# One-hots of the second neighbour sum: from two ScalarE steps to one GpSimd comparison

## What is computed

```python
def _rgcn(x, edge_index, edge_type, weight, root, bias):
    src, dst = (edge_index[0], edge_index[1])
    msgs = x[src]
    out = x @ root + bias
    for r in range(weight.shape[0]):
        mask = (edge_type == r).astype(x.dtype)
        sums = jax.ops.segment_sum(msgs * mask[:, None], dst, num_segments=n)
        cnt = jax.ops.segment_sum(mask, dst, num_segments=n)
        mean = sums / jnp.maximum(cnt, 1.0)[:, None]
        out = out + mean @ weight[r]
    return out
u = _rgcn(x, edge_index, edge_type, weight, root, bias)
z = jnp.concatenate([u, x], axis=1) @ w_gate + b_gate
h = jnp.tanh(u) * z + x * (1.0 - z)
```

## Time and profile before

| What | us |
|---|---|
| Median of 3 runs (2558.67, 2566.13, 2567.54) | 2566.13 |
| Span of the profiled execution (first to last instruction) | 2555.3 |
| TensorE busy in that span | 2387.4 |
| VectorE, ScalarE, GpSimd busy | 1562.8, 919.0, 871.2 |
| The second neighbour sum, first gather to last slot | about 1724 to 2130 |

### The profile page before, as it was taken

How to read it: one execution, slowest core, us unless ns; L and a number is a source line. 1 busy time by engine, 2 the same in 40 slices (tenths; PEclk the granted TensorE clock), 3 DMA queues, 4 the chain that set the end, 5 groups by cost and what they waited for, 6 DMA issues and landing times.

```text
span 2555.3 us, 29106 instructions
## 1 busy us (share of the span) xinstructions
PE 2387.4 (93%) x9625; PEld 1691.6 (66%) x9625; DVE 1562.8 (61%) x2417; ACT 919.0 (36%) x1629; POOL 871.2 (34%) x843
## 2 busy tenths in 40 slices
PE   6989998969999979999999999999999897986998
PEld 3543334634444458788888888888778686875786
DVE  8737777431142377645545545547889898766655
ACT  4012223311111233222222212217889896534333
POOL 2767774001111035555600000014445552112444
PEclk9999999979999989999999999999999998997999
DMA  4026776273342265453453353357778885447875
GB/s 156 2 97 205 206 208 170 107 260 111 99 132 98 72 224 221 166 191 131 140 202 124 135 209 124 127 185 251 245 257 297 280 298 209 158 149 272 313 278 192
DMA packets 195724, 466.10 MB, mean 182 GB/s; under 512 B 29353, under 2 KB 30153, under 8 KB 195609
## 3 DMA queue, kind: packets, MB, share of 16 engines
q1 hardware_dynamic: 101192, 219.34, 24.6%
q0 software_dynamic: 64272, 190.20, 23.2%
q10 hardware_dynamic: 30144, 55.12, 5.7%
HBM read 370.23 MB, written 99.96 MB: 184 GB/s over the span
## 4 chain that ended last, share of the span: by engine, by line
PE 82%; DMA 7%; DVE 5%; issue 2%; ACT 2%; POOL 1%; DVEq 0%; SPq 0%; ACTq 0%; POOLq 0%
PE pair L1292 9%; PE pair L1293 8%; PE pair L1294 8%; PE pair L1172 6%; PE pair L1192 6%; PE pair L1079 4%; PE pair L1310 3%; PE pair L1313 3%; PE pair L1330 3%; PE pair L1332 3%; PE pair L1331 3%; PE pair L1039 3%; PE pair L1058 3%; DMA XT<-h_rows,l_src 2%; PE pair L1017 2%
## 5 line engine op out<-in xcount | busy, mean ns | idle before, releaser
L1471 ACT ACTIVATE sq_h<-quad 128x512 fp32r<-128x512 f32 x196 | 122.9, 633 | 453.6 <-PE pair L1294 448.8
L1292 PE MATMUL pair<-sq_h,xh 128*128 128x512 f32 x700 | 273.5, 391 | 4.3 <-DVE sq_l L2290 4.3
L1293 PE MATMUL pair<-sq_h,xl 128*128 128x512 f32 x700 | 273.2, 390 | 0.0
L1294 PE MATMUL pair<-sq_l,xh 128*128 128x512 f32 x700 | 273.1, 390 | 0.0
L932 POOL DMA_INDIRECT rows_y<-y_rows,l_row x184 | 201.2, 1093 | 206.0 <-PE pair L1313 178.9
L2378 DVE SCALAR_TENSOR_TENSOR low_y<-rows_y,l_inv,high_y 128x1024 fp32r<-128x1024 f32 x184 | 233.8, 1283 | 41.3 <-ACT high_y L1471 41.0
L1471 ACT ACTIVATE high_y<-rows_y,l_inv 128x1024 fp32r<-128x1024 f32 x184 | 210.4, 1143 | 35.7 <-PE pair L1313 25.7
L909 POOL DMA_INDIRECT inv_ring<-inv_count,at_ring x184 | 189.0, 1027 | 74.6 <-issue 56.3
L872 POOL DMA_INDIRECT XT<-h_rows,l_src x184 | 178.6, 971 | 68.5 <-issue 37.2
L2290 DVE TENSOR_TENSOR sq_l<-quad,sq_h 128x512 fp32r<-128x512 f32 x196 | 131.5, 696 | 99.3 <-ACT sq_h L1471 98.5
L1079 PE MATMUL pair<-XT,XN 128*128 128x504 f32 x368 | 188.5, 636 | 0.0
(11 more groups left out here) (369 smaller groups left out, 5037.7 us busy)
## 6 DMA issues: line engine op xcount, KB each, us to landing
quad<-in_L_gnn_weight SPq DMA_DIRECT2D x28, 1024.0 KB, 5.6
xh<-sum_parts SPq DMA_DIRECT2D x14, 1280.0 KB, 7.4
xl<-sum_parts SPq DMA_DIRECT2D x14, 1280.0 KB, 11.0
y_rows<-u ACTq DMA_DIRECT2D x70, 256.0 KB, 2.2
tok_raw<-in_L_ffn_w SPq DMA_DIRECT2D x8, 2048.0 KB, 13.6
tok_raw<-in_L_ffn_w SPq DMA_DIRECT2D x16, 1024.0 KB, 13.0
exp_bg<-bias_gelu_rows SPq DMA_DIRECT2D x23, 512.0 KB, 5.0
x_rows<-X SPq DMA_DIRECT2D x20, 512.0 KB, 6.4
```

The costliest lines, as they stand in the source:

```text
L1292: mm(o, high[:, k, :], sq_h[:, k, :], start=(k == 0), stop=False)
L1293: mm(o, low[:, k, :], sq_h[:, k, :], start=False, stop=False)
L1294: last = mm(o, high[:, k, :], sq_l[:, k, :], start=False, stop=(k == KE - 1))
L1471: return nc.scalar.activation(dst, src, func, **kw)
```

## The change

ScalarE's lines 1728 and 1736 go, with `row_off`, its semaphore and its waits. GpSimd makes the one-hot of a slot with one instruction, `tensor_scalar` with `is_equal`: the column numbers `iota_free` compared with the slot's target row. It stands in front of the gather of the slot three further on, behind the wait that the gather had already; the last three stand behind all gathers. Sizes of rings, the gathers and the work of TensorE and VectorE are unchanged.

```diff
-        high_ready, low_ready, row_off_ready, hot01_ready = sem("high_ready"), sem("low_ready"), sem("row_off_ready"), sem("hot01_ready")
+        high_ready, low_ready, hot01_ready = sem("high_ready"), sem("low_ready"), sem("hot01_ready")
...
+            def one_hot(s):
+                if s >= HOTS:
+                    pool.wait_ge(slot_summed, RING0 + SLOTS + s - HOTS + 1)
+                pool.tensor_scalar(hot01[:, s % HOTS, :], iota_free[:, 0:P], l_row[:, s:s + 1], None, ALU.is_equal).then_inc(hot01_ready, 1)
+
             for s in range(SLOTS):
                 if s >= RING1:
                     pool.wait_ge(slot_summed, RING0 + SLOTS + s - RING1 + 1)
+                if s >= HOTS - 1:
+                    one_hot(s - HOTS + 1)
                 pool.indirect_dma_start(rows_y[s % RING1][:], None, y_rows,
                                         bass.IndirectOffsetOnAxis(ap=l_row8[:, s:s + 1], axis=0)
                                         ).then_inc(y_in[s % RING1], 16)
+            for s in range(SLOTS - HOTS + 1, SLOTS):
+                one_hot(s)
...
             for s in range(SLOTS):
-                if s >= 1:
-                    act.wait_ge(hot01_ready, s)
-                nc.scalar.activation(row_off[:], iota_free[:, 0:P], ACT.Abs, bias=l_row[:, s:s + 1], scale=-1.0).then_inc(row_off_ready, 1)
                 act.wait_ge(*y_here(s))
                 if s >= 3:
                     act.wait_ge(slot_summed, RING0 + SLOTS + s - 2)
                 copy(high_y[s % 3][:], rows_y[s % RING1][:], scale=l_inv[:, s:s + 1]).then_inc(high_ready, 1)
-                act.wait_ge(row_off_ready, s + 1)
-                if s >= HOTS:
-                    act.wait_ge(slot_summed, RING0 + SLOTS + s - HOTS + 1)
-                nc.scalar.activation(hot01[:, s % HOTS, :], row_off[:], ACT.Relu, bias=ones[:, 0:1], scale=-1.0).then_inc(hot01_ready, 1)
```

More of the change, by code:

```diff
@@ L269, in build @@
         gate0_half = place("gate0_half", "hot", [P, HALF], skip=HOTS * P)
-        row_off = place("row_off", "sel", [P, P])
         uh = place("uh", "w", [P, 2, KD, P], F32R)
```

## The result

| | before | after |
|---|---|---|
| Median of 4 runs, us | 2566.4 | 2623.5 |
| Lowest and highest | 2558.7, 2567.5 | 2619.2, 2636.9 |
| Span of the profiled execution | 2555.3 | 2622.9 |

The changed kernel is slower: its time is 1.023 of that before, 95% interval 1.0194 to 1.0266, or 57 us. The interval is clear of 1; whether the loss is above 2% it leaves open. The forecast was 2591.1, 25 us slower. The sign held, and GpSimd is the bound as forecast; the size was off by more than a factor of two.

The account below looks back on a forecast made before the run. TensorE was taken to bound the stage before, GpSimd units 2 and 3 after: 26 us lost less 1 gained makes 25; the span of 2555.3 becomes 2580.3, plus 10.8 for the median gives 2591.1 us, range 2562 to 2637.

Parts of the forecast that it names:

- What bounds, what it removes: Sum stage: TensorE bounds, GpSimd looks idle; dropping ScalarE's two steps gains 1 us, at unit changes and in units 2, 3.
- What it adds: GpSimd: 184 comparisons of 128 columns at 0.29 us, upper bound 0.45; with 0.15 us issue gap, 0.44 us per slot.
- What holds it: GpSimd: each comparison waits for a running low_y, 0.41 us on average, 0.35 in longer slots; 42 of 184 gathers already held.
- The sum per slot: GpSimd's need against spare time: units 2 and 3 over by 0.26 and 0.37 us per slot, 11 and 16.5 us, taken as 26.
- Unit 1 fits, and unit 0: GpSimd in units 0 and 1: unit 1's need of 0.80 us per slot fits its spare 0.99, unit 0 likewise; no loss.
- The range: Whole kernel time from 2562 to 2637 us, taking in most of the no-change case and the lower part of the heavy one.
- heavy rival: Second rival, GpSimd: comparison 0.45 us, gather held as often, 0.41 us more; 70 to 75 us slower, some 2637; chance 0.15.
- No change: First rival: GpSimd and VectorE fall into step, or queues absorb holds; -1 to +10 us, some 2570; chance 0.36 including fourth rival.
- Queues of three and four slots: Part of the no-change rival: slots saved up between GpSimd, ScalarE and TensorE absorb the holds on GpSimd.
- Faster: Third rival: ScalarE's lateness caused all TensorE waits outside the cover and GpSimd keeps up; -14.8 us, 2551; chance 0.03.
- The signs to look for: Units 2 and 3: gathers well over 1.09 us or comparisons far over 0.3, GpSimd not waiting for sums, high_y waiting for gathers.
- The last sign: GpSimd: comparisons of 0.6 us or more that nothing holds would point to the second, heavier rival.

Follow-up runs that it names:

- memset run: Changed kernel with GpSimd's comparison replaced by a memset of the same 128 columns, one-hots left all zeros: 2557.4 us against 2565.0 before, stage 396.5 us.
- first trace of before: The kernel before, unedited, in its first profiled trace: stage of the sum 397.7 us; a later repeat on the third chip gave 407.4.
- copy run: Changed kernel with the comparison replaced by a 128-column copy, one-hots left out: stage 419.1 us, whole 2736.8 us against 2723.9 before on that chip.
- first pair of traces: Kernel before and changed kernel, unedited, first traced: stages 397.7 and 468.6 us; the second pair, repeated on the third chip, gave 407.4 and 466.2.
- one-input run: Changed kernel with low_y made from rows_y alone, subtraction left out, so that step has one SBUF input: 2575.7 us against 2565.0 before, stage 401.8.
- VectorE's one-hots: Kernel with one-hots made by VectorE in front of low_y, ScalarE's two steps gone, GpSimd only gathering: 2720.3 us against 2723.9 before, ratio 0.9993, stage 403.0.

## Why the prediction was right in its reasons and wrong in its size

- **What bounds, what it removes.** Right as far as it can be seen: inside a unit TensorE waited for nobody, and freeing ScalarE gave next to nothing. The memset run's stage is 1 us shorter than the first trace of before, well inside the spread, so the 1 us itself is not shown.
- **What it adds.** This is the step that failed: "I take 0.29", with 0.45 as the upper bound. The comparison takes 0.61 us, above both. The row of the select was one instruction of another form, the copies were another form too, and I took the two-input sum as a ceiling by its slope per column, though the changed form has a fixed part of its own. A smaller miss is in the gather: behind a comparison it takes 1.01 us unheld, not 0.94 (behind a memset 0.94, behind a copy 0.96). A third goes the other way and was hidden: the working takes 0.30 us in front of each gather and 0.15 behind the comparison, 0.45 in all, but a gather that follows a comparison no longer follows a gather. Measured are 0.17 and 0.04, so 0.24 us per slot were counted too much.
- **What holds it.** Right in kind. The hold was put at 0.35 to 0.41 us per comparison; measured are 1.03 - 0.61 = 0.42. That is nearer than the rule behind it deserves: at the 2.53 us that a slot took, a chance arrival would give 1.31/2.53 x 0.63 = 0.33 us. Arrivals are not by chance; in the copy run they made the hold 0.57. The gathers are held 0.27 us on average, where they were held 0.16 before; I had them unchanged. The count of 42 gathers needs a word: by the recorded times 126 start inside a `low_y`. Those that start 0.13 to 0.98 us into it are the 42, and each ends 0.81 us behind its end; 14 that start in its first 0.07 us and 70 that start in its last 0.15 us are not held.
- **The sum per slot.** With 0.61 in place of 0.29, and 0.07 more for the gather, the same working gives for units 2 and 3 an excess of 0.26 + 0.32 + 0.07 = 0.65 and 0.76 us, so 50 x 0.65 - 2 = 30.5 and 50 x 0.76 - 2 = 36 us, and for units 0 and 1, 0.80 + 0.39 - 0.99 = 0.20 us, 3.6 and 5.6 us: 76 us in all against 71 measured in the first pair of traces and 59 in the second. By units it fits less well: measured are 24.9 and 26.9, 8.5 and 9.2. Part of the agreement is luck. The 0.24 us of gaps counted too much stand against 0.07 us of hold on the comparison and 0.11 on the gather that are missing; with all three units 2 and 3 come to an excess of 0.59 and 0.70 us, 27.5 and 33 us. And with the right gaps but the price of 0.29 and the holds as forecast, unit 2 would have been over by 0.02 us and unit 3 by 0.13 us, and the forecast would have been close to no change. With the copy, whose length was the one I used, the stage was 419.1 us, 12 to 21 above the two of before, where the sum had 25: there, too, a hold of 0.57 us in place of 0.35 made up for the gaps. "Unit 1 fits, and unit 0" fell with the comparison's price.
- **The range.** The time lies inside it, above the 2579 to 2615 us that I had given the forecast. Its upper end, 2637, is the heavy rival, which had a longer comparison; but its 0.45 us was still too short, and its other half, a gather held as often as the comparison, came out at 0.27 us in place of 0.41. It is the nearest of the four, and I had given it 0.15.
- **The other rivals.** No change was what the stages of the one-input run and of VectorE's one-hots gave (401.8 and 403.0 us); it needed either no holds or another engine. Queues of three and four slots did absorb the gathers' holds in the memset run, but not both holds and the comparison. Faster falls: without ScalarE's two steps and with one-hots for nothing, TensorE still waited 18.1 of 19.2 us for `low_y`.
- **The signs to look for.** They were there: gathers of 1.28 us, comparisons far over 0.3, hardly a wait of GpSimd for sums, `high_y` waiting for the gather's DMA. The last sign was there as well, the one of the second rival, for the comparison takes 0.61 us where nothing holds it.

## What to carry to other kernels

Before work goes to an idle engine, price the very form of the instruction, with its operands and size, by a probe: another form of the same size was off by a factor of two here, and the sum hung on it. Then ask who shares something with that engine: idle time per turn has to hold the new instruction and the holds it will meet, and here the comparison's length without holds cost next to nothing (one-input run), a short instruction with its holds 12 to 21 us (copy), both together 59 to 71 us. Count also what the gaps between instructions become when their order changes. Where a GpSimd instruction must run beside VectorE steps with two inputs in SBUF, try cutting these steps shorter: in this kernel one trace showed most of the loss gone.

## What the runs showed of the hardware

- On GpSimd a `tensor_scalar` of 128 columns takes 0.61 us (0.53 with a constant), for both operations tried and with its output rounded or not (0.60); a copy of the same size takes 0.29, a memset 0.21.
- A VectorE step with two tensor inputs in SBUF holds GpSimd's comparisons, copies and gathers until 0.13 us before its recorded end (held comparisons end 0.48 us behind it, held gathers of the kernel before 0.81); a gather that starts in its first 0.07 us is not held (14 in the kernel before). The same columns with one input in SBUF hold none of 184 gathers (1.03 us at most), and of 184 memsets, which read nothing, none was held in the memset run (0.23 us at most).
- The other direction is cheap here: `low_y` took 1.31 us on average in the changed kernel in place of 1.28, though 184 comparisons of 0.61 us ran beside it.
- A gather takes 1.01 us behind a comparison on GpSimd, starting 0.17 us after it; behind another gather, a memset or a copy it takes 0.94, 0.94 and 0.96.
